# Local head attention on one core: the last block's odd score tiles masked on TensorE and gathered by a maximum

## The chip, the cores and the metric

One core of one Trainium2 chip runs the whole program in one launch. The metric is the device time in microseconds (us). The engines are named as the profile names them: PE (TensorE; PEld is its weight load), DVE (VectorE), ACT (ScalarE), POOL (GpSimd) and SP (SyncE, which here only issues DMAs).

## The reference, cut to what matters

The program computes two transformer layers: attention against a context, a mixture of experts, a second attention and a feed-forward. Only the second attention matters here. It does not attend over the sequence: for each of 2048 tokens, each of 16 heads (32 wide) attends to the 16 heads of the same token.

```python
B, S, D, H = (4, 1024, 512, 16)
HD = D // H
bs, sl, nf = q.shape
Q = (q @ Wq.T + bq).reshape(bs, sl, H, HD)
K = (k @ Wk.T + bk).reshape(bs, sl, H, HD)
V = (v @ Wv.T + bv).reshape(bs, sl, H, HD)
score = jnp.einsum('bshd,bsgd->bshg', Q, K)
weight = jax.nn.softmax(score, axis=-1)
attn = jnp.einsum('bshg,bsgd->bshd', weight, V).reshape(bs, sl, nf)
return attn @ Wo.T + bo
```

## The kernel before, in words

Four stages follow each other: `l0_attention`, `l0_experts`, `l1_attention` and `l1_output_ffn`, each a block of five instruction streams that ends with all engines joined. The change lies in `l1_attention`, the merged stage: it projects K, V and Q and does the attention in the same loop.

The tokens are cut into NBLK = 4 blocks of 512. A block has NP = 8 pairs of units, so there are 32 pairs, p = 0 to 31. A unit is one quarter of the block (a quadrant of 32 partitions, which holds the 32 features of a head) and UN = 4 groups of TOK = 8 tokens. For one group, a matmul over 32 rows multiplies 8 tokens x 16 heads of queries by 8 tokens x 16 heads of keys: a 128 x 128 tile, of which only the entries with the same token are wanted, one in eight. The two units of a pair lie in two neighbouring quadrants and write two PSUM banks, `sc_ps[:, 0]` and `sc_ps[:, 1]`, the even and the odd tile, each 128 x 512.

The stream of each engine is written out by hand. For pair p:

- PE, `scores(p)` (L2140): eight matmuls of 32 rows, even and odd in turn. They wait for the masking of both tiles of pair p-1, since there is one pair of banks. Then come half of a projection, `turn` (L2149, eight transposes of the probabilities of pair p-2), the other half of a projection, and `weigh` (L2162, pair p-3).
- DVE, `own_scores(2p)`: multiply the even tile by the 0/1 mask (L2248), then sum over the 8 tokens (L2254), which leaves 16 scores per row. Then `normalise(p-1)` (L2266 sum, L2268 reciprocal, L2270 scaling), then `own_scores(2p+1)` for the odd tile, then `subtract_max(p)` (L2259, L2261).
- ACT: the exponentials (L2024) and the copies of the turned probabilities and of the outputs out of PSUM.
- POOL, `expand(2p-2)` and `expand(2p-1)` (L1931): spread the normalised weights back to a 128 x 512 tile.

Beside blocks 0 to 2, that is beside pairs 0 to 23, PE also does the projections of the next block; some of these items need DVE too (`h_low_part`, L2223, and `take_v`, L2230). Beside the last block's pairs, 24 to 31, there are none. Pair 24 waits for the last block's queries, which come back by DMA and are laid out by ACT (L2014).

In this kernel's profile the rows of `scores` show two records for each matmul: an fp32 product is issued as two, so eight matmuls are x16. A transpose is one record.

The wait that stands between DVE and PE, and the two instructions around it:

```python
if p:
    pe.wait_ge(s_masked, 2 * p)
...
dve.tensor_tensor(masked_sc[:], sc_ps[:, u % 2], mask..., ALU.mult).then_inc(s_masked, 1)
...
dve.tensor_reduce(own_sc[:, p % 3, u % 2], masked_sc..., AX.X, ALU.add).then_inc(s_gathered, 1)
```

Of the kernel before, what the change touches and what calls it, by code (L numbers as in the profile page):

```python
# [14 lines left out]
P = 128  # L15
F32 = mybir.dt.float32
F32R = mybir.dt.float32r
I32 = mybir.dt.int32
ALU = mybir.AluOpType
ACT = mybir.ActivationFunctionType  # L20
AX = mybir.AxisListType
# [1529 lines left out]
def l1_attention(nc, new_sem, x_shared, expert_out, place, weight, carry, ctxT, W, w_ffn, woT, x2, qT, kT, vT, aT, sums):  # L1551
    T, D = x2.shape
    KC = D // P
    NBLK = T // BLK
    HD = 32
# [9 lines left out]
    RING = 6  # L1565
    TURN_LAG, LAG = 2, 3
# [20 lines left out]
    WHICH = {"k": 0, "v": 1, "q": 2}  # L1587

# [8 lines left out]
    with ExitStack() as c:  # L1597
        def sb(name, shape, dt=F32):
            return c.enter_context(nc.sbuf_tensor("p_" + name, shape, dt))

        def sem(name):
            return new_sem("p_" + name)
# [28 lines left out]
        ones = sb("ones", [P, P])  # L1631
        mhalf = sb("mhalf", [P, 1])
# [3 lines left out]
        masked_sc = sb("masked_sc", [P, UN, P])  # L1636
        own_sc = sb("own_sc", [P, 3, 2, UN, H])
# [42 lines left out]
        s_masked = sem("s_masked")  # L1680
        s_gathered = sem("s_gathered")
# [218 lines left out]
        def _(pool):  # L1900
# [40 lines left out]
            for n in range(TPB):  # L1941
                gather(n)
            for n in range(TPB):
                w_low("q", n)
                power(n)
# [136 lines left out]
        def _(pe):  # L2082
# [46 lines left out]
            def scores(p):  # L2129
                b, w = p // NP, p % NP  # L2130
                if w == 0:
                    pe.wait_ge(k_in[b % 2], IN_QK * (b // 2 + 1))
                    pe.wait_ge(q_moved, b + 1)
                if p:
                    pe.wait_ge(s_masked, 2 * p)
                for y in range(UN):
                    for u in (2 * w, 2 * w + 1):
                        rows = slice(u % NQ * HD, (u % NQ + 1) * HD)
                        n = u // NQ * UN + y
                        mm = pe.matmul(sc_ps[:, u % 2, y, :], q_laid[rows, b % 2, n],  # L2140
                                       k_sb[rows, b % 2, :, n * TOK:(n + 1) * TOK], start=True, stop=True)
                mm.then_inc(s_ready, 1)
# [39 lines left out]
        def _(dve):  # L2182
# [59 lines left out]
            def own_scores(u):  # L2242

                p = u // 2
                dve.wait_ge(s_ready, p + 1)
                if u:
                    dve.wait_ge(s_gathered, u)
# [5 lines left out]
                dve.wait_ge(s_masked, u + 1)  # L2253
# [10 lines left out]
            def normalise(p):  # L2264
# [6 lines left out]
                                  ALU.mult).then_inc(e_done, 1)  # L2271

# [39 lines left out]
            for p in range(NP * NBLK):  # L2312
# [13 lines left out]
                item_part(2 * p + 1)  # L2326
                for m in pieces_beside(p, "dve"):
                    sum_piece(m)
# [513 lines left out]
```

## Time and profile before

| | us |
|---|---|
| median of 3 runs | 2047.57 (2047.14 to 2050.84) |
| the profiled execution's own time | 2048.61 |
| its span, first to last instruction | 2046.8 |
| PE busy | 1918.5 (94% of the span) |
| DVE busy | 987.4 (48%) |
| last block's pairs, first score to end of the stage's PE work | 1678.6 to 1723.6 |

Busy shares are averages over four stages with different limits. The stretch that the change touches is about 45 us of 2047, so it is read by itself: which engine waits for which in it.

### The profile page before, as it was taken

Reading aid. Unit: us, or ns where it says so; the run is one execution under the profiler, and the core shown is the slowest. Engines: PE = TensorE matmul, PEld = TensorE weight load, DVE = VectorE, ACT = ScalarE, POOL = GpSimd, SP = SyncE. Lnnn points to the kernel's source line nnn. Section 1 sums busy time; section 2 is a strip of 40 time slices with the busy share of each in tenths; the row PEclk is TensorE's granted clock in tenths of the full one; section 3 lists DMA queues with packets and bytes.
Section 4 is the critical chain, followed back from the end, with each engine's and each line's share of the span. In section 5 each row is a group of like instructions: output and inputs, shape, how many; then the busy total and the mean of one; then the engine's idle time right before and its main releaser. Section 6 shows DMA issues by size and latency. Waiting matters only on the chain. (4 is left out here: it accounts for less than half of the span.)

```text
span 2046.8 us, 29418 instructions
## 1 busy us (share of the span) xinstructions
PE 1918.5 (94%) x10300; PEld 1608.7 (79%) x10300; DVE 987.4 (48%) x1657; ACT 752.6 (37%) x1144; POOL 1114.2 (54%) x996
## 2 busy tenths in 40 slices
PE   6999999999999999979999799998989896899998
PEld 5889888988898888857777699997767774678886
DVE  2447444745465545653332133334778866782111
ACT  3336333633345332622121222212445544343433
POOL 6775688648855876444117845640544424843333
PEclk9999999999999999979999899999989998999999
DMA  4231332223222323334126655532888655430000
GB/s 150 103 113 53 114 107 99 73 78 131 101 81 84 124 103 103 125 118 161 49 101 230 219 167 173 148 105 79 243 250 220 189 143 163 141 114 31 20 20 20
DMA packets 172235, 248.10 MB, mean 121 GB/s; under 512 B 44944, under 2 KB 69520, under 8 KB 172112
## 3 DMA queue, kind: packets, MB, share of 16 engines
q1 hardware_dynamic: 157024, 202.09, 31.1%
q0 software_dynamic: 9472, 34.09, 5.1%
q10 hardware_dynamic: 5616, 10.23, 1.3%
q8 instruction: 85, 1.39, 0.3%
q14 instruction: 38, 0.31, 0.1%
HBM read 179.77 MB, written 66.58 MB: 120 GB/s over the span
## 5 line engine op out<-in xcount | busy, mean ns | idle before, releaser
L257 POOL TENSOR_TENSOR a_w_hl<-a_w_raw,a_w_hl 128x512 fp32r<-128x512 f32 x236 | 312.7, 1357 | 142.9 <-ACT a_w_hl L330 142.7
L455 PE MATMUL a_proj<-a_c_hl,a_w_hl 128*128 128x512 f32 x768 | 179.8, 394 | 21.8 <-DVE a_w_hl L576 19.9
L455 PEld LDWEIGHTS a_proj<-a_c_hl,a_w_hl 128*128 128x128 f32 x768 | 144.4, 189 | 53.4 <-issue 21.5
L455 PE MATMUL a_proj<-a_w_hl,a_c_hl 128*128 128x512 f32 x768 | 181.2, 392 | 0.0
L529 PE MATMUL a_proj<-a_w_hl,a_a_hl 128*128 128x512 f32 x768 | 178.5, 391 | 0.0
L455 PE MATMUL a_proj<-a_a_hl,a_w_hl 128*128 128x512 f32 x768 | 176.4, 390 | 0.0
L330 ACT ACTIVATE a_w_hl<-a_w_raw 128x2048 fp32r<-128x2048 f32 x60 | 114.8, 1914 | 152.0 <-PE a_proj L455 106.7
L356 ACT ACTIVATE a_sq<-a_proj,a_vecs 128x512 f32<-128x512 f32 x128 | 88.2, 691 | 218.6 <-PE a_proj L455 136.6
L455 PEld LDWEIGHTS a_proj<-a_a_hl,a_w_hl 128*128 128x128 f32 x768 | 143.6, 188 | 29.7
L2530 POOL TENSOR_TENSOR f_a_hl<-f_act_sb,f_a_hl 128x512 fp32r<-128x512 f32 x64 | 86.0, 1344 | 148.6 <-ACT f_a_hl L2578 148.5
L529 PEld LDWEIGHTS a_proj<-a_w_hl,a_a_hl 128*128 128x128 f32 x768 | 143.0, 188 | 29.0
L455 PEld LDWEIGHTS a_proj<-a_w_hl,a_c_hl 128*128 128x128 f32 x768 | 142.4, 188 | 28.6
L1316 PE MATMUL b_gate_up<-b_wts,b_xt_hl 128*128 x936 | 160.0, 327 | 4.2 <-DVE b_xt_hl L1525 4.2
L1316 PEld LDWEIGHTS b_gate_up<-b_wts,b_xt_hl 128*128 128x128 f32 x936 | 155.2, 191 | 8.2 <-issue 5.0
L288 POOL TENSOR_TENSOR a_ssum<-a_ssum,a_sq 128x512 f32<-128x512 f32 x112 | 145.5, 1299 | 28.4 <-ACT a_sq L356 21.3
L1222 PE MATMUL b_gate_up<-b_wts 128*128 128x512 f32 (+1 forms) x576 | 136.0, 394 | 0.0
L1931 POOL TENSOR_TENSOR p_probs<-p_own_sc,p_mask 128x512 f32<-128x512 f32 x64 | 67.8, 1081 | 108.9 <-DVE p_own_sc L2270 107.7
L1222 PEld LDWEIGHTS b_gate_up<-b_wts 128*128 128x128 f32 (+1 forms) x576 | 102.9, 179 | 29.4
L2638 PE MATMUL f_totals<-f_ternary,f_a_hl 128*128 128x512 f32 x512 | 122.5, 396 | 0.0
L2624 PE MATMUL f_hidden<-f_h_hl,f_ternary 128*128 x512 | 120.4, 393 | 0.0
L2638 PEld LDWEIGHTS f_totals<-f_ternary,f_a_hl 128*128 128x128 f32 x512 | 96.4, 188 | 23.3
L632 DVE SCALAR_TENSOR_TENSOR a_a_hl<-a_qT,a_vecs,a_a_hl 128x512 fp32r<-128x512 f32 x64 | 67.4, 1068 | 96.3 <-ACT a_a_hl L370 96.3
(258 smaller groups left out, 3523.8 us busy)
## 6 DMA issues: line engine op xcount, KB each, us to landing
a_w_raw<-in_a_ki_w SPq DMA_DIRECT2D x16, 1024.0 KB, 5.6
a_w_raw<-in_a_vi_w SPq DMA_DIRECT2D x16, 1024.0 KB, 4.9
a_w_raw<-in_a_q_w SPq DMA_DIRECT2D x16, 1024.0 KB, 4.9
a_w_raw<-in_a_o_w SPq DMA_DIRECT2D x16, 1024.0 KB, 5.3
spare<-in_b_gate_up POOLq DMA_DIRECT2D x32, 352.0 KB, 4.1
l_sorted_rows<-b_zeros SPq DMA_DIRECT2D x39, 256.0 KB, 3.2
spare<-l_sorted_rows SPq DMA_DIRECT2D x39, 256.0 KB, 3.2
l_expert_out<-spare ACTq DMA_DIRECT2D x39, 256.0 KB, 3.5
```

Of the source, the lines that this page charges most:

```text
L257: ins = pool.tensor_tensor(w_hl[:, s, 1, k], w_raw[:, s, k], f32(w_hl[:, s, 0, k]), ALU.subtract)
L288: pool.tensor_tensor(ssum[:], first, sq[:, n % 2, :], ALU.add).then_inc(sq_added, 1)
L330: act.activation(w_hl[:, i % 2, 0], w_raw[:, i % 2], ACT.Copy).then_inc(w_high, 1)
L356: act.activation(sq[:, n % 2, :], proj[:, j, :], ACT.Square, bias=bias)\
L455: mm = pe.matmul(proj[:, j, :], left, right, start=(k == 0 and n == 0), stop=(k == KC - 1 and n == 2))
L529: mm = pe.matmul(proj[:, j, :], a_hl[:, ap, k, j * P:(j + 1) * P], w_hl[:, i % 2, wp, k], start=(n == 0 and m == 0), stop=(n == 4 * G - 1 ...
L1222: mm = pe.matmul(gu_ps[0:w, n, part, :], gu_hl[:, s, wp, k, cols], h_hl[:, hslot, ap, k, :], start=(k == 0 and m == 0), stop=(k == KC - 1 ...
L1316: mm = pe.matmul(gu_ps[:, i % 2, half, 0:F], x_part(i, xp)[:, own], part(r, P, at, F), start=(k == 0 and xp == 0 and start == HI), stop=(k ...
L1931: pool.tensor_tensor(probs[:, u % RING].rearrange("p y (g t) -> p y g t", t=TOK), own_sc[:, p % 3, u % 2].unsqueeze(3).to_broadcast([P, UN ...
L2530: pool.tensor_tensor(a_hl[:, 1, m % FC, :], act_sb[:, m % 2, :], f32(a_hl[:, 0, m % FC, :]), ALU.subtract).then_inc(g_split, 1)
L2624: mm = pe.matmul(h_ps[:, m % 2, :], w_t[:, 2 * g, k, f * P:(f + 1) * P], h_hl[:, ap, k, bass.ds(BLK * t, BLK)], start=(k == 0 and ap == 0) ...
L2638: mm = pe.matmul(y_ps[:, j, :], a_hl[:, ap, f, j * P:(j + 1) * P], w_t[:, 2 * g + 1, f, :], start=(m == 0 and ap == 0), stop=(m == NG * FC ...
```

## The change

From pair 24 on (`LEAN = NP * (NBLK - 1)`), the pairs that have no projections beside them, the odd tile is masked by PE. After the two score matmuls of a group, a third one adds `same_tok` x `not_tok` to the odd tile: over the 32 rows of that quadrant it adds 0 where the tokens agree and -1e30 where they do not (only 8 of the 32 rows of `same_tok` are not zero). DVE then needs no multiplication for the odd tile: one maximum over the 8 tokens, read straight from PSUM, gives the 16 scores. PE's next scores wait for that maximum (`s_gathered`) in place of the multiplication (`s_masked`). The even tile is treated as before. The two constant tiles are made in unused room: POOL writes row numbers early in the stage, and DVE makes the rest in four instructions behind pair 16.

```diff
+    LEAN = NP * (NBLK - 1)
...
+        low_row, low_flag = ones[:, 0:1].bitcast(I32), ones[:, 1:2]
...
+        same_tok, not_tok = (routed[:, 0, r, 0:P] for r in range(2))
...
+            pool.wait_ge(const_made, 4)
+            pool.iota(low_row, pattern=[[0, 1]], base=0, channel_multiplier=1).then_inc(off_tok, 1)
...
-                if p:
+                if p > LEAN:
+                    pe.wait_ge(s_gathered, 2 * p)
+                elif p:
                     pe.wait_ge(s_masked, 2 * p)
+                if p == LEAN:
+                    pe.wait_ge(off_tok, 5)
...
-                                       k_sb[rows, b % 2, :, n * TOK:(n + 1) * TOK], start=True, stop=True)
+                                       k_sb[rows, b % 2, :, n * TOK:(n + 1) * TOK], start=True,
+                                       stop=p < LEAN or u % 2 == 0)
+                    if p >= LEAN:
+                        mm = pe.matmul(sc_ps[:, 1, y, :], same_tok[rows], not_tok[rows], start=False, stop=True)
...
+                if p >= LEAN and u % 2:
+                    dve.wait_ge(p_ready, 2 * (p - 3) + 2)
+                    dve.tensor_reduce(own_sc[:, p % 3, 1], sc_ps[:, 1].rearrange("p y (g t) -> p y g t", t=TOK),
+                                      AX.X, ALU.max).then_inc(s_gathered, 1)
+                    return
...
-                dve.wait_ge(s_masked, u + 1)
+                dve.wait_ge(s_masked, u + 1 if p < LEAN else LEAN + p + 1)
...
+            def make_off_tok():
+                dve.wait_ge(off_tok, 1)
+                dve.tensor_scalar(low_row, low_row, HD - TOK, None, ALU.bitwise_and).then_inc(off_tok, 1)
+                dve.wait_ge(off_tok, 2)
+                dve.tensor_scalar(low_flag, low_row, 0.0, None, ALU.is_equal).then_inc(off_tok, 1)
+                dve.wait_ge(off_tok, 3)
+                as_rows = mask[:].rearrange("p h t -> p (h t)")
+                dve.tensor_scalar(same_tok, as_rows, low_flag, None, ALU.mult).then_inc(off_tok, 1)
+                dve.tensor_scalar(not_tok, as_rows, 1.0, BIG, ALU.subtract, ALU.mult).then_inc(off_tok, 1)
...
+                if p == LEAN - NP:
+                    make_off_tok()
```

DVE's order in the last block, before: two tiles with the same two instructions each, `normalise` between them.

```order
L2248 TENSOR_TENSOR p_masked_sc<-p_scores,p_mask 128x512
L2254 TENSOR_REDUCE p_own_sc<-p_masked_sc 128x64
L2266 TENSOR_REDUCE p_den<-p_own_sc 128x8
L2268 RECIPROCAL p_rden<-p_den 128x8
L2270 TENSOR_TENSOR p_own_sc<-p_own_sc,p_rden 128x128
L2248 TENSOR_TENSOR p_masked_sc<-p_scores,p_mask 128x512
L2254 TENSOR_REDUCE p_own_sc<-p_masked_sc 128x64
L2259 TENSOR_REDUCE p_mx<-p_own_sc 128x8
L2261 TENSOR_TENSOR p_own_sc<-p_own_sc,p_mx 128x128
```

The same place after the change (the numbers are lines of the changed file).

```order
L2267 TENSOR_TENSOR p_masked_sc<-p_scores,p_mask 128x512
L2273 TENSOR_REDUCE p_own_sc<-p_masked_sc 128x64
L2285 TENSOR_REDUCE p_den<-p_own_sc 128x8
L2287 RECIPROCAL p_rden<-p_den 128x8
L2289 TENSOR_TENSOR p_own_sc<-p_own_sc,p_rden 128x128
L2262 TENSOR_REDUCE p_own_sc<-p_scores 128x64
L2278 TENSOR_REDUCE p_mx<-p_own_sc 128x8
L2280 TENSOR_TENSOR p_own_sc<-p_own_sc,p_mx 128x128
```

One of nine instructions is gone; the one that frees the odd bank, L2262, stands where the multiplication stood. DVE's order behind pair 16, after the change:

```order
L2237 TENSOR_TENSOR p_a_hl<-p_proj,p_a_hl 128x4x128 x2
L2294 TENSOR_SCALAR p_ones<-p_ones 128x1
L2296 TENSOR_SCALAR p_ones<-p_ones 128x1
L2299 TENSOR_SCALAR p_routed<-p_mask,p_ones 128x128
L2300 TENSOR_SCALAR p_routed<-p_mask 128x128
L2267 TENSOR_TENSOR p_masked_sc<-p_scores,p_mask 128x512
```

The four middle instructions are new; before, pair 17's mask (the last row) came right behind `h_low_part` (the first row). PE's order in one pair of the last block, after the change; before, there was one row `p_scores<-p_k,carry` with x8, and nothing with `p_routed`.

```order
L2151 MATMUL p_scores<-p_k,carry 128x128 x2
L2155 MATMUL p_scores<-p_routed 128x128
L2151 MATMUL p_scores<-p_k,carry 128x128 x2
L2155 MATMUL p_scores<-p_routed 128x128
L2151 MATMUL p_scores<-p_k,carry 128x128 x2
L2155 MATMUL p_scores<-p_routed 128x128
L2151 MATMUL p_scores<-p_k,carry 128x128 x2
L2155 MATMUL p_scores<-p_routed 128x128
```

Four matmuls of 32 rows are added to each of eight pairs, in the odd tile's quadrant, between the even and odd ones of the next group.

## Rows read from the trace of the kernel before

**Rows 1.** Windows: length, busy of PE, PEld, DVE, ACT, POOL (count); granted clock; DMA.

```profile
1679.00:1689.00 10.00, 10.00 (x72) 8.21 (x72) 6.76 (x15) 4.67 (x13) 2.50 (x3) 0.50 0.63 175
1690.80:1713.20 22.40, 16.50 (x205) 13.34 (x204) 20.67 (x47) 10.32 (x26) 10.54 (x10) 1.00 0.56 163
```

**Rows 2.** Timeline, DVE, pair 28: start us, us, what, [idle before].

```profile
1699.75 0.68 DVE L2248 TENSOR_TENSOR p_masked_sc<-p_scores,p_mask 128x512 f32<-128x512 f32 x1
1700.53 0.69 DVE L2254 TENSOR_REDUCE p_own_sc<-p_masked_sc 128x64 f32<-128x512 f32 x1
...
1701.90 0.68 DVE L2248 TENSOR_TENSOR p_masked_sc<-p_scores,p_mask 128x512 f32<-128x512 f32 x1
1702.68 0.69 DVE L2254 TENSOR_REDUCE p_own_sc<-p_masked_sc 128x64 f32<-128x512 f32 x1
...
1704.23 0.68 DVE L2248 TENSOR_TENSOR p_masked_sc<-p_scores,p_mask 128x512 f32<-128x512 f32 x1
```

**Rows 3.** Timeline, PE, pairs 29 and 30.

```profile
1702.63 1.16 PE L2140 MATMUL p_scores<-p_k,carry 32*128 32x128 f32 x16 [1.25 <-DVE p_masked_sc L2248]
1703.73 1.15 PE L2149 MATMUL p_turned<-p_ident,p_probs 128*128 128x128 f32 x8
1704.81 1.07 PE L2162 MATMUL p_out<-p_probs,p_v 128*32 128x128 f32 x16
1707.11 1.16 PE L2140 MATMUL p_scores<-p_k,carry 32*128 32x128 f32 x16 [1.24 <-DVE p_masked_sc L2248]
```

**Rows 4.** Timeline, DVE and PE, pair 21: scores and the mask behind them.

```profile
1659.45 0.69 DVE L2248 TENSOR_TENSOR p_masked_sc<-p_scores,p_mask 128x512 f32<-128x512 f32 x1 [0.77 <-PE p_scores L2140]
...
1658.24 1.16 PE L2140 MATMUL p_scores<-p_k,carry 32*128 32x128 f32 x16
```

**Rows 5.** Timeline, PE, `l0_attention`: fp32 matmuls of all 128 rows, one after another.

```profile
838.40 1.06 PE L516 MATMUL a_proj<-a_probs,carry 128*128 128x128 f32 x8
839.30 1.06 PE L495 MATMUL a_scores<-spare,a_qT 128*128 128x128 f32 x8
```

**Rows 6.** Timeline, PE, pairs 24 to 26, the start of the last block.

```profile
1678.61 1.87 PE L2140 MATMUL p_scores<-p_k,carry 32*128 32x128 f32 x16 [2.53 <-issue]
...
1684.16 2.08 PE L2140 MATMUL p_scores<-p_k,carry 32*128 32x128 f32 x16
1686.17 1.97 PE L2149 MATMUL p_turned<-p_ident,p_probs 128*128 128x128 f32 x8
```

**Rows 7.** Timeline, DVE, even masks of pairs 24, 25 and 26.

```profile
1680.52 0.69 DVE L2248 TENSOR_TENSOR p_masked_sc<-p_scores,p_mask 128x512 f32<-128x512 f32 x1 [4.03 <-PE p_scores L2140]
...
1686.29 0.69 DVE L2248 TENSOR_TENSOR p_masked_sc<-p_scores,p_mask 128x512 f32<-128x512 f32 x1 [1.20 <-PE p_scores L2140]
...
1690.79 0.68 DVE L2248 TENSOR_TENSOR p_masked_sc<-p_scores,p_mask 128x512 f32<-128x512 f32 x1
```

**Rows 8.** Groups, DVE, whole span: busy us, mean ns, idle before.

```profile
L642 DVE TENSOR_REDUCE a_mx<-a_scores 128x4 f32<-128x512 f32 x64 | 43.9, 686 | 5.7 <-PE a_scores L495 5.7
L2254 DVE TENSOR_REDUCE p_own_sc<-p_masked_sc 128x64 f32<-128x512 f32 x64 | 43.9, 686 | 6.2
```

**Rows 9.** Groups as in 8: small operations like the four new ones.

```profile
L2209 DVE TENSOR_SCALAR p_rstd<-p_mv 128x1 f32<-128x1 f32 x16 | 2.5, 154 | 0.6
L2283 DVE TENSOR_SCALAR p_mask<-p_flag 128x128 f32<-128x128 f32 x1 | 0.2, 228 | 0.0
```

**Rows 10.** Timeline, PE and DVE, pairs 17 and 18.

```profile
1636.06 2.99 PE L2125 MATMUL p_proj<-p_a_hl,p_w_hl 128*128 128x512 f32 x12 [2.70 <-DVE p_a_hl L2223]
...
1628.54 0.69 DVE L2223 TENSOR_TENSOR p_a_hl<-p_proj,p_a_hl 128x512 fp32r<-128x512 f32 x1 [0.26 <-ACT p_a_hl L1997]
1629.31 0.69 DVE L2248 TENSOR_TENSOR p_masked_sc<-p_scores,p_mask 128x512 f32<-128x512 f32 x1
```

**Rows 11.** Timeline, the tail: pair 31's even mask and its spreading.

```profile
1713.19 0.68 DVE L2248 TENSOR_TENSOR p_masked_sc<-p_scores,p_mask 128x512 f32<-128x512 f32 x1
...
1719.06 2.11 POOL L1931 TENSOR_TENSOR p_probs<-p_own_sc,p_mask 128x512 f32<-128x512 f32 x2 [1.46 <-DVE p_own_sc L2270]
```

More of the change, by code:

```diff
@@ L1565, in l1_attention @@
     RING = 6
+    BIG = 1e30
     TURN_LAG, LAG = 2, 3
@@ L1680, in l1_attention @@
         s_masked = sem("s_masked")
+        off_tok = sem("off_tok")
         s_gathered = sem("s_gathered")
```

## The prediction

> **What bounds the kernel now.** The program ends on TensorE's work in its last stage, so a delay or a saving in the merged stage moves the whole time only if it moves that stage's end. It does: the next stage starts when all engines have joined, and nothing of it overlaps. So I read the last block's pairs, 24 to 31, alone. First the windows: from 1690.80 to 1713.20, five periods of a pair, DVE is busy 20.67 of 22.40 us and PE 16.50, at a granted clock of 1.00 (2.4 GHz) [rows 1]. Then the timeline of one pair: on DVE the even mask starts at 1699.75, the odd at 1701.90, the next pair's even mask at 1704.23, so a pair takes 4.48 us, with no idle time in brackets [rows 2]. On PE the scores wait 1.25 and 1.24 us for DVE [rows 3]. DVE sets the pace, and PE's wait costs nothing, because the scores of the next pair (start 1702.63) are done before DVE is back at 1704.23. That overlap is what the reader should keep in view: PE starts 0.73 us after the odd mask starts, and DVE then still has the sum, the maximum and the subtraction to do, 1.55 us from 1702.68 to 1704.23.
>
> The block begins otherwise. From 1679 to 1689 the granted clock was 0.50 (1.2 GHz) with PE busy all 10.00 us [rows 1]; pair 24's scores start at 1678.61, pair 25's at 1684.16 [rows 6], and DVE waits for PE, 4.03 and 1.20 us. There PE is the bound. Even masks start at 1680.52, 1686.29 and 1690.79 [rows 7].
>
> **The change, part by part.**
>
> *The multiplication of the odd tile goes.* DVE's own work per pair falls by the step from the odd mask to the sum, 1701.90 to 1702.68, or 0.78 us [rows 2], to 3.70. If DVE stayed the bound that would be a gain of 8 x 0.78 = 6.2 us.
>
> *The maximum from PSUM.* No row of this stage reads PSUM with a reduction, but the first attention does: 686 ns, the same as the sum from SBUF [rows 8]. I take 0.69. The Trainium skill, VectorE: DVE Perf Modes, section on the TRN2 errata, gives a PSUM source 62 cycles more than an SBUF source; worked out at its 0.96 GHz that would be an estimate of 0.06 us more per pair, 0.5 us in eight. The rows show no difference, so I leave it out.
>
> *The wait moves.* The odd bank was free when the mask ended; now it is free when the maximum ends. The maximum stands where the mask stood, 2.15 us behind the even mask, and has the same length, so PE's scores start at the same place, 2.15 + 0.74 = 2.89 us behind the even mask. But what DVE has left to do after that has shrunk by the 0.78, to about 0.8 us, and PE now needs longer. The scores are no longer hidden, and the two engines take turns: a loop of DVE (2.89), then PE, then DVE.
>
> *PE's part.* From the start of the scores to the even mask behind them, where DVE was waiting, it is 1659.45 - 1658.24 = 1.21 us [rows 4]. The four added matmuls are two records each. What a record costs in one row group is seen in the first attention: eight records, 838.40 to 839.30, so 0.112 us each [rows 5]. Sixteen records of scores take 1.10 us to the next operation [rows 3], which is possible only if the two quadrants run side by side, two records at a time. The added records all fall to the odd quadrant, behind the two they add to. In program order the even quadrant can fill only one of their places, as it filled one of the odd scores' before. So eight more places, 8 x 0.112 = 0.90 us per pair. At the lower clock twice that, 1.79: sixteen score records there take 2.01 us to the next operation, against 1.10 [rows 6, 3].
>
> *The steady loop:* 2.89 + 1.21 + 0.90 = 5.00 us against 4.48, so 0.52 more for each of the five steps from pair 26 to 31: +2.6 us. PE's own work is 1.10 + 1.08 + 1.07 [rows 3] + 0.90 = 4.15 us, so it does not bind by itself.
>
> *The four DVE instructions behind pair 16.* 0.154 twice and 0.228 twice [rows 9] with some 0.03 us for each wait: 0.9 us. Pair 17's mask follows `h_low_part` at 1629.31 with no idle time before it, and PE then waits 2.70 us for DVE's `h_low_part` at 1636.06 [rows 10]. Behind that PE is the bound up to the queries of block 3, on which pair 24 waits. So I count the whole 0.9 as a shift of pair 24, to 1679.51. Low bound 0, if something else comes last there. The row numbers on POOL are one instruction of 128x1 ahead of work that waits for DVE; I count nothing, at most 0.2.
>
> *The start of the block.* Pair 24: mask at 1679.51 + 1.91 + 1.79 = 1683.21. PE, busy without a gap, starts pair 25 after 5.55 + 1.79 us, at 1686.85. If the clock comes back at about 1689.1 as before, 2.3 of the 3.92 us (2.13 + 1.79) are at the low clock and the rest costs half: mask 25 at 1690.0. Then the loop: scores 26 at 1692.9, mask 26 at 1695.0. Before it was 1690.79, so +4.2 us, with the 0.9 in it.
>
> *The end.* Pair 31's even mask comes at 1713.19 + 4.2 + 2.6 = 1720.0. From there to the spreading on POOL it was 5.87 us [rows 11]; the missing multiplication makes it 0.78 shorter. What follows is as before.
>
> **Sum:** +4.2 + 2.6 - 0.8 = +6.0 us. Against the profiled execution's own 2048.61 us that is 2054.6; the median of the runs lies 1.04 lower, so 2053.6 us, slower by 0.29%. A measurement of this kernel can tell about 0.2%, 4.1 us, from no change.
>
> **Bounds of PE's part.** It is the one large unknown. Lower: an added matmul costs half, 0.45 us per pair; then the loop is 4.55 (+0.3 in all), mask 26 comes at 1693.5 (+2.7), and the end is +2.2, or 2049.8. Upper: the two quadrants stop overlapping, 24 records of 0.112 in place of eight places, +1.8 us per pair; loop 5.9, and the end is some +13, or 2061. I take 0.90, which is counted from the nearest rows on both sides.
>
> **The rivals.**
>
> - *PE hides the mask (not slower).* At the place where DVE waits for `s_ready`, all hangs on how much longer the scores take. If they grow by less than 0.38 us per pair, the loop (4.10 + that) is shorter than 4.48. At nothing added, mask 26 comes +0.5, five steps give -1.9, the end -0.8: -2.2 us, 2045.4. For it: the rows show two quadrants side by side, and the even one stands idle while the odd is masked. Against it: the added work is all in one quadrant, whose sixteen records need 16 x 0.112 = 1.79 us whatever the other does. Even DVE as the sole bound (3.70) gives only about -4 us, since the block's start is PE's.
> - *The clock comes back earlier.* In the low stretch PE was already busy 10.00 of 10.00 us, so more matmuls cannot fill a gap; but they put other work in it. If pair 25's scores run at the full clock, mask 25 comes 1.0 us earlier: +5.0, or 2052.6. It is in my range. The Trainium skill, TensorE: Matmul & The Clock Gate, Part 1, says that the throttled state is the default and that activity releases it; by that rule a denser stage leans this way, never to a gain against before.
> - *Overlap lost (slower by far).* 2061, as above. Nothing in the rows speaks for it except that three matmuls in a row now change quadrant unevenly.
> - *The masking does not happen in time.* Pair 24 waits for the constants, but the order has them behind pair 16, some 50 us earlier; no cost.
>
> **How the numbers follow.** My forecast, DVE and PE in turns at about 5.0 us a pair, 0.62; an earlier clock 0.12; a cheaper mask between 0 and the lower bound 0.16, of which the greater part ends within 0.2%; overlap lost 0.06; other effects of either sign, the next stage's clock among them, 0.04. Range: 2049.5 to 2058. Its low end takes in the lower bound; its high end is 4.4 us above the sum, which is a third of the way to the lost overlap, 0.6 us more per pair. Outside are most of the lost overlap and the fully hidden mask. Slower by over 0.2% (above 2051.7) 0.76, within 0.2% 0.20, faster 0.04.
>
> **What the profile after would show.** Right: in the last block L2262 takes 0.69 us; PE's scores are x24, 2.0 us at the full clock, and start with DVE as their releaser; DVE has a new idle time of about 1.3 us per pair before the even mask, ended by PE scores; the masks are 5.0 us apart. Wrong: masks 4.5 us or less apart, or no idle time of DVE there, would say that the added matmuls ran beside the others. Pair 24 starting at the old place, measured from pair 16, would say that the four instructions were hidden.

## The result, and the profile after

| | before | after |
|---|---|---|
| median, us | 2047.93 (2047.14 to 2050.84, 6 runs) | 2057.59 (2055.31 to 2063.09, 6 runs) |
| ratio, 95% interval | | 1.0044 [1.0034, 1.0054] |
| profiled execution, its time | 2048.61 | 2055.76 |
| its span | 2046.8 | 2054.0 |
| PE busy | 1918.5 | 1928.0 |
| DVE busy | 987.4 | 979.4 |

The change made the kernel slower: 9.7 us between the medians, 9.0 us by the ratio with an interval of about 7 to 11 us, and 7.15 us between the two profiled executions. The ratios, here and below, are worked out over the fast executions alone, without the few slow ones (up to 7242 us), and are not the quotients of the medians. DVE works 8 us less and the program takes longer. The median came out 4 us above the predicted 2053.6 and inside the range, close to its high end.

First the windows of the kernel after: from pair 26's even mask to pair 31's, then the low stretch at the block's start, then a short stretch inside the block (columns as in [rows 1]).

```profile
1695.40:1720.91 25.51, 21.86 (x241) 18.74 (x242) 16.48 (x40) 9.87 (x23) 10.78 (x10) 0.93 0.61 186
1681.10:1688.00 6.90, 6.85 (x44) 6.18 (x46) 2.82 (x7) 2.38 (x6) 0.71 (x1) 0.51 0.51 116
1705.00:1708.40 3.40, 3.40 (x21) 2.71 (x22) 2.67 (x6) 1.56 (x4) 0.53 (x1) 0.50 0.66 159
```

Against [rows 1], DVE fell from 20.67 of 22.40 us to 16.48 of 25.51, PE rose from 16.50 to 21.86, and neither is busy all the time. That is how two engines look when they wait for each other in turn. The clock shows 0.93 where before it was 1.00; the last row is the reason, and it returns below.

DVE's timeline of the kernel after, the pairs that answer to [rows 2]:

```profile
1695.40 0.69 DVE L2267 TENSOR_TENSOR p_masked_sc<-p_scores,p_mask 128x512 f32<-128x512 f32 x1 [1.45 <-PE p_scores L2155]
...
1700.38 0.69 DVE L2267 TENSOR_TENSOR p_masked_sc<-p_scores,p_mask 128x512 f32<-128x512 f32 x1 [1.45 <-PE p_scores L2155]
...
1702.54 0.69 DVE L2262 TENSOR_REDUCE p_own_sc<-p_scores 128x64 f32<-128x512 f32 x1
1703.26 0.29 DVE L2278 TENSOR_REDUCE p_mx<-p_own_sc 128x8 f32<-128x128 f32 x1
...
1705.55 0.69 DVE L2267 TENSOR_TENSOR p_masked_sc<-p_scores,p_mask 128x512 f32<-128x512 f32 x1 [1.63 <-PE p_scores L2155]
```

Even masks are 4.98 us apart (1695.40 to 1700.38) where they were 4.48. The odd maximum L2262 starts 2.16 us behind the even mask and takes 0.69 us, as the odd mask did. Before, none of the masks in [rows 2] had a bracket; now each even mask has one that ends with PE's scores, 1.45 us where the clock is full.

PE's timeline beside it, which answers to [rows 3]; a record x5 is scores, the next line is the mask matmul behind them:

```profile
1698.29 0.59 PE L2151 MATMUL p_scores<-p_k,carry 32*128 32x128 f32 x5 [0.91 <-DVE p_own_sc L2262]
...
1699.96 0.38 PE L2155 MATMUL p_scores<-p_routed 32*128 32x128 f32 x2
1700.28 1.09 PE L2163 MATMUL p_turned<-p_ident,p_probs 128*128 128x128 f32 x8
1701.30 1.07 PE L2176 MATMUL p_out<-p_probs,p_v 128*32 128x128 f32 x16
...
1703.28 0.59 PE L2151 MATMUL p_scores<-p_k,carry 32*128 32x128 f32 x5 [0.92 <-DVE p_own_sc L2262]
```

From the first score to the turning behind it, 1698.29 to 1700.28, is 1.99 us, against 1.10 in [rows 3]: 0.89 us more. And PE, which is now the later one, itself waits 0.91 us for DVE's odd maximum. From the even mask to PE's scores it is 2.89 us, and from those to the next even mask 2.09, together 4.98: a pair is one lap of a chain that goes once through each engine.

Where the four constants are made, DVE (answers to [rows 10]):

```profile
1629.20 0.69 DVE L2237 TENSOR_TENSOR p_a_hl<-p_proj,p_a_hl 128x512 fp32r<-128x512 f32 x1 [0.26 <-ACT p_a_hl L2004]
1629.81 0.14 DVE L2294 TENSOR_SCALAR p_ones<-p_ones 128x1 int32<-128x1 int32 x1
1629.98 0.15 DVE L2296 TENSOR_SCALAR p_ones<-p_ones 128x1 f32<-128x1 int32 x1
1630.17 0.29 DVE L2299 TENSOR_SCALAR p_routed<-p_mask,p_ones 128x128 f32<-128x128 f32 x1
1630.37 0.22 DVE L2300 TENSOR_SCALAR p_routed<-p_mask 128x128 f32<-128x128 f32 x1
1630.51 0.68 DVE L2267 TENSOR_TENSOR p_masked_sc<-p_scores,p_mask 128x512 f32<-128x512 f32 x1
```

The mask starts 1.31 us behind `h_low_part` instead of 0.77 [rows 10]: the four instructions delay it by 0.54 us, not by 0.9, because their ends overlap. Last, PE and DVE of the kernel after from pair 18 to the start of the block (answers to [rows 10, 6, 7]):

```profile
1637.26 4.35 PE L2132 MATMUL p_proj<-p_a_hl,p_w_hl 128*128 128x512 f32 x12 [2.70 <-DVE p_a_hl L2237]
...
1681.15 0.98 PE L2151 MATMUL p_scores<-p_k,carry 32*128 32x128 f32 x5 [2.52 <-issue]
...
1684.97 0.69 DVE L2267 TENSOR_TENSOR p_masked_sc<-p_scores,p_mask 128x512 f32<-128x512 f32 x1 [5.94 <-PE p_scores L2155]
...
1690.41 0.69 DVE L2267 TENSOR_TENSOR p_masked_sc<-p_scores,p_mask 128x512 f32<-128x512 f32 x1 [1.89 <-PE p_scores L2155]
```

Pair 24's scores start 2.54 us later than before (1678.61 [rows 6]), and only 0.54 of that belongs to the four instructions. `h_low_part` ahead of them already starts 0.66 us late (1629.20 against 1628.54), and pair 18's projection took 4.35 us in place of 2.99, since a stretch of low clock fell on it: 1.36 us. So differences between two single profiles carry an error of a microsecond or more. At pair 26's even mask the delay is 4.61 us (1695.40 against 1690.79), at pair 31's 7.72 (1720.91 against 1713.19 [rows 11]), and the program's end is 7.2 us later.

### The profile page after: what moved, and what is told of

Read it like the earlier page. It is cut to its first block and busy times, and to the rows that moved or that the text cites. A ratio compares the mean times of both kernels' runs of the same rounds, so it can differ in the third digit from the quotient of the medians.

```text
span 2054.0 us, 29535 instructions
## 1 busy us (share of the span) xinstructions
PE 1928.0 (94%) x10364; PEld 1618.9 (79%) x10364; DVE 979.4 (48%) x1653; ACT 752.8 (37%) x1144; POOL 1120.0 (55%) x997
```

## The experiments

Each ran beside the kernel before on the same chip; the ratios are against those runs. The medians of before were 2047.93 beside the change; 2048.07 beside constants alone, matmuls only, no matmuls and constants late; 2047.30 beside matmuls twice and the three bf16 kernels; 2048.65 beside the other four. **Lap** is the distance between even masks (or even maxima) at the full clock. **Five steps** runs from the maximum over the heads (`p_mx`) of pair 26 to that of pair 31, and **low** is how much of it was at the granted clock 0.50. Kernels that make the constants "late" make them behind pair 23 in place of pair 16.

| kernel | lap | five steps | low | median, us | ratio, 95% interval |
|---|---|---|---|---|---|
| before | 4.48 | 22.41 | 0 | 2047.93 | |
| constants alone | 4.48 | 22.41 | 0 | 2047.99 | 1.0003 [0.9993, 1.0013] |
| the change | 4.98 | 25.52 | 3.4 | 2057.59 | 1.0044 [1.0034, 1.0054] |
| the change again | 4.98 | 26.13 | 6.8 | 2056.05 | 1.0040 [1.0026, 1.0054] |
| matmuls only | 4.98 | 26.14 | 6.8 | 2056.69 | 1.0044 [1.0031, 1.0057] |
| constants late | 4.98 | 25.96 | 3.5 | 2053.15 | 1.0036 [1.0022, 1.0051] |
| same quadrant, other bank, late | 4.98 | 25.51 | 3.4 | 2052.80 | 1.0019 [1.0005, 1.0032] |
| matmuls twice | 5.87 | 35.01 | 20.5 | 2066.82 | 1.0093 [1.0068, 1.0118] |
| no matmuls | 4.10 | 20.50 | 0 | 2046.22 | 0.9989 [0.9980, 0.9998] |
| other quadrant, other bank, late | 4.12 | 22.42 | 3.4 | 2045.43 | 0.9982 [0.9969, 0.9994] |
| odd tile in bf16, late | 4.48 | 22.36 | 0 | 2048.74 | 1.0008 [0.9993, 1.0023] |
| both tiles in fp32, late | 4.20 | 21.02 | 0 | 2045.94 | 0.9987 [0.9977, 0.9998] |
| both tiles in bf16, late | 3.68 | 24.54 | 10.2 | 2043.83 | 0.9980 [0.9968, 0.9991] |
| both tiles in bf16, wide, late | 3.52 | 17.58 | 0 | 2041.90 | 0.9970 [0.9956, 0.9983] |

### The parts alone: constants, matmuls, moved wait

The constants alone, on top of the kernel before:

```diff
-    LEAN = NP * (NBLK - 1)
+    LEAN = NP * NBLK
...
-                if p == LEAN - NP:
+                if p == LEAN - 2 * NP:
```

> The kernel before with the constant tiles alone: POOL's row numbers and DVE's four instructions behind pair 16, no added matmul, no maximum, no moved wait. My theory: DVE's 0.8 to 0.9 us go onto the path of pair 17 and 18, PE's wait for DVE before the projection stays 2.7 us and comes 0.9 us later, and pair 24 starts 0.9 us later; the loop of the last block stays 4.48 us; in all +0.9 us, some 2048.8. Rival, the four instructions are hidden: pair 24 at the old distance from pair 16 and no change. Rival, the clock: the shift puts other work in a stretch at the lower clock, and pair 24 comes 2 us or more later in some execution though the instructions take 0.9.

Measured: no difference that can be told from zero, 1.0003 [0.9993, 1.0013]. The timeline has the same 0.5 us of delay for pair 17, and here too pair 18's projection took 4.37 us at the low clock, with the block unchanged. The 0.5 us, and the expected 0.9, lie inside that interval (-1.4 to +2.7 us), so they are neither shown nor excluded in the total. The constants' place is not what made the change lose 9 us.

The mask matmuls alone, from pair 24 (`MASKED`) on, with DVE doing all its old work (the multiplication then acts on an already masked tile):

```diff
-                                       stop=p < LEAN or u % 2 == 0)
-                    if p >= LEAN:
+                                       stop=p < MASKED or u % 2 == 0)
+                    if p >= MASKED:
```

> The changed kernel with DVE's old work: the mask matmuls are added to the odd tile, but DVE multiplies it by the mask and sums as before, and PE waits for the multiplication (the output is the same, since -1e30 is multiplied by 0). My theory (DVE and PE in turns): PE starts 2.88 us behind the even mask and needs 2.11, so the masks are 4.99 us apart, as in the changed kernel, DVE idles some 0.5 us per pair in place of 1.45, and only the end is later, by 0.78 us: some 0.8 us above the changed kernel, 2058.4. Rival, DVE's saved instruction is worth its length in every pair: 8 x 0.78 = 6.2 us above the changed kernel, 2063.8, masks 5.8 us apart.

DVE's timeline of this kernel:

```profile
1694.36 0.69 DVE L2268 TENSOR_TENSOR p_masked_sc<-p_scores,p_mask 128x512 f32<-128x512 f32 x1 [1.58 <-PE p_scores L2156]
...
1696.51 0.68 DVE L2268 TENSOR_TENSOR p_masked_sc<-p_scores,p_mask 128x512 f32<-128x512 f32 x1
...
1699.34 0.69 DVE L2268 TENSOR_TENSOR p_masked_sc<-p_scores,p_mask 128x512 f32<-128x512 f32 x1 [0.41 <-PE p_scores L2156]
```

The lap is 4.98 us, the same as in the full change, and the ratio is the same 1.0044. DVE has 0.78 us more to do per pair and still waits, 0.41 us. Taking that instruction away turned work into idle time and saved nothing per pair: it stands behind the release of PE and beside PE's scores. The 0.8 us at the end that were expected on top of the change are less than these runs can tell (median 2056.69 against 2057.59 and 2056.05).

The other half alone, the odd maximum and the moved wait without the matmuls:

```diff
-                    if p >= LEAN:
-                        mm = pe.matmul(sc_ps[:, 1, y, :], same_tok[rows], not_tok[rows], start=False, stop=True)
```

> The changed kernel without the mask matmuls: the odd tile's maximum is taken over unmasked scores, so the masking of the odd tile is left out. The wait stands where the change put it. My theory: the masks are 2.89 + 1.21 = 4.10 us apart, DVE idles some 0.4 us per pair, and the end is 2 us before the kernel before: 2045.7. Rival, the moved wait costs by itself: masks 4.5 us apart or more, 2048 or above. Rival, the low clock and not the matmuls makes the loss: still above 2050.

```profile
1692.22 0.69 DVE L2265 TENSOR_TENSOR p_masked_sc<-p_scores,p_mask 128x512 f32<-128x512 f32 x1 [0.56 <-PE p_scores L2151]
...
1696.32 0.69 DVE L2265 TENSOR_TENSOR p_masked_sc<-p_scores,p_mask 128x512 f32<-128x512 f32 x1 [0.56 <-PE p_scores L2151]
```

This kernel leaves the odd tile unmasked; only its time counts. DVE's timeline shows a lap of 4.10 us, which is 2.89 + 1.21, and even here DVE waits 0.56 us. So the wait for the maximum costs nothing, and the largest gain that this rearrangement could have had at no price for PE is 0.38 us a pair. The matmuls are the loss, 0.88 us a pair.

### The constants late

```diff
-                if p == LEAN - NP:
+                if p == LEAN - 1:
```

> The changed kernel with DVE's four constant instructions behind pair 23, where DVE idles 4 us or more before pair 24. My theory: pair 24's scores start at the old 1678.6 (from the same start of the stage), and the whole is 0.9 us shorter than the changed kernel in its mechanism, some 2056.7; the loop stays 4.98. Rival, the four instructions were hidden where they stood: no difference. Rival, the clock: since the changed kernel's profile has 1.36 us lost to a low clock in a projection of pair 18, removing the shift could give back 2.3 us, 2055.3.

Measured: 1.0036 [1.0022, 1.0051], lap 4.98. The interval overlaps those of the change, so what the constants' place is worth stays below what these runs can tell.

### What an added matmul costs: doubled, moved, narrowed

Each mask matmul issued twice:

```diff
-                        mm = pe.matmul(sc_ps[:, 1, y, :], same_tok[rows], not_tok[rows], start=False, stop=True)
+                        for last in (False, True):
+                            mm = pe.matmul(sc_ps[:, 1, y, :], same_tok[rows], not_tok[rows], start=False, stop=last)
```

> The changed kernel with every mask matmul issued twice (the mask becomes -2e30; the output is the same). My theory: eight more places of 0.112 us in the odd quadrant, so the masks are 4.98 + 0.90 = 5.88 us apart at the full clock; DVE idles 2.35 us per pair; in all some 8 us above the changed kernel (five loops of 0.9, the rest at the block's start at the lower clock), near 2066. Rival, only the first mask matmul's latency counts, or the second runs beside the even quadrant: less than 0.5 us more per pair, under 2062.

```profile
1690.19 0.69 DVE L2268 TENSOR_TENSOR p_masked_sc<-p_scores,p_mask 128x512 f32<-128x512 f32 x1 [3.26 <-PE p_scores L2156]
...
1696.06 0.69 DVE L2268 TENSOR_TENSOR p_masked_sc<-p_scores,p_mask 128x512 f32<-128x512 f32 x1 [2.34 <-PE p_scores L2156]
```

DVE's timeline: 5.87 us, again 0.89 more, and DVE's wait grew by the same 0.89, from 1.45 to 2.34. Over none, four and eight added matmuls (laps 4.10, 4.98, 5.87) the price is linear in their number. The median of 2066.82 us is the expected 2066, but this profile also has 20.5 us of low clock in its five steps.

Is it a price of the quadrant, of the PSUM bank, or of a matmul as such? Two kernels write the same product into a bank that the last block does not use, so both leave the odd tile unmasked. One takes the rows of a quadrant without scores, as in this cut; the other keeps the odd tile's quadrant:

```diff
-                        mm = pe.matmul(sc_ps[:, 1, y, :], same_tok[rows], not_tok[rows], start=False, stop=True)
+                        off = slice((u + 2) % NQ * HD, ((u + 2) % NQ + 1) * HD)
+                        mm = pe.matmul(proj[:, 0, y * P:(y + 1) * P], same_tok[off], not_tok[off], start=True, stop=True)
```

> The four mask matmuls of a pair are issued as in the change, but on the rows of a quadrant that holds no scores of this pair, and they write a PSUM bank that the last block does not use (the projections'), so their product reaches nothing: the odd tile's maximum is unmasked. The constants are made behind pair 23. My theory is that the 0.90 us is the queue in one quadrant, not a cost of the matmuls as such: eight records in a third quadrant then run beside the other sixteen, PE's part falls back to about 1.21 us, and the loop is 2.89 + 1.21 = 4.10 us, as without the mask matmuls, at most 0.2 more; total near 2046. Rival: a matmul costs its place wherever it stands (only two run side by side, or the issue is the limit), so the loop stays 4.98 us and the total near 2053 to 2056.

> As the kernel with the other quadrant, but on the odd tile's own quadrant, still into the unused PSUM bank; the odd tile's maximum is unmasked and the constants are made behind pair 23. It differs from the change only in the bank that the mask matmuls write and in that they add to nothing. My theory, a queue in one quadrant: loop 4.98 us, total near 2053. Rival, the cost is that of adding to a bank that was just written: a different bank then takes it away, and the loop is near 4.10 us.

PE's timeline with the other quadrant:

```profile
1708.08 0.38 PE L2151 MATMUL p_scores<-p_k,carry 32*128 32x128 f32 x2 [0.83 <-DVE p_own_sc L2263]
1708.10 0.37 PE L2156 MATMUL p_proj<-p_routed 32*128 32x128 f32 x1
1708.30 0.28 PE L2151 MATMUL p_scores<-p_k,carry 32*128 32x128 f32 x2
...
1709.18 1.09 PE L2164 MATMUL p_turned<-p_ident,p_probs 128*128 128x128 f32 x7
```

And with the odd tile's own quadrant, also on PE:

```profile
1695.74 0.59 PE L2151 MATMUL p_scores<-p_k,carry 32*128 32x128 f32 x5 [0.91 <-DVE p_own_sc L2263]
...
1697.42 0.38 PE L2156 MATMUL p_proj<-p_routed 32*128 32x128 f32 x2
1697.73 1.09 PE L2164 MATMUL p_turned<-p_ident,p_probs 128*128 128x128 f32 x8
```

In the other quadrant, 24 records take 1.10 us from the first score to the turning, exactly what 16 took before [rows 3]: three run at a time, the mask record starting 0.02 us behind the scores'. The lap is 4.12 us and the kernel is faster than before. In the same quadrant, with the bank changed, the scores take 1.99 us to the turning and the lap stays at 4.98 us. So the 0.89 us is the queue in one quadrant. It is neither a price of adding to a bank nor one of issuing a matmul. The Trainium skill, TensorE: Matmul & The Clock Gate, Part 3 (The mechanism), has matmuls on distinct row groups run concurrently and end in program order. The trace agrees with the first half, by the 24 records in 1.10 us; it can't show the second, since the ends of matmuls in these profiles are modelled. The third quadrant may not be able to serve the change itself, which has to add to the odd tile's own bank. The Trainium skill, TensorEngine Tiling (Array Packing), Gotcha 1, says that different row tiles cannot access the same PSUM bank at once; no run here tried that.

The constants as bf16 make a mask matmul one record in place of two (late, odd tile alone):

```diff
-        same_tok, not_tok = (routed[:, 0, r, 0:P] for r in range(2))
+        same_tok, not_tok = (routed[:, 0, r, 0:P // 2].bitcast(BF16) for r in range(2))
```

> The changed kernel with the two constant tiles in bf16 (0, 1 and -1e30 lose nothing that matters), and made behind pair 23. The mask matmul is then one record of half the length. My theory, places filled strictly in program order: a mask matmul still waits for the odd scores and holds back the next even ones, so it takes one place of 0.112 in place of two: 0.45 us per pair, masks 4.54 us apart, the whole about 1.5 us above the kernel before, 2049.6. Rival, only its own length counts (0.056 each): 4.32 us apart, and under the kernel before by 0.5 us. Rival, the number of matmuls counts and not their length: 4.98.

```profile
1696.33 0.59 PE L2152 MATMUL p_scores<-p_k,carry 32*128 32x128 f32 x5 [0.91 <-DVE p_own_sc L2263]
...
1697.66 0.21 PE L2156 MATMUL p_scores<-p_routed 32*128 32x128 bf16 x1
1697.81 1.09 PE L2164 MATMUL p_turned<-p_ident,p_probs 128*128 128x128 f32 x8
```

PE's scores take 1.48 us to the turning: four bf16 matmuls cost 0.38 us, or 0.095 each, where the fp32 ones cost 0.22 each. That is neither the one place of 0.112 that was expected nor the rival's 0.056, but nearer to the place. The lap is 2.89 + 1.59 = 4.48, equal to the kernel before by coincidence, and so is the time: 1.0008 [0.9993, 1.0023]. This is the break-even of the idea for one tile, and it lies where the prediction's rival had put it, 0.38 us a pair.

### Both tiles masked on PE

If the price is places in one quadrant, the even tile's mask matmuls should be free beside the odd ones, and DVE would lose both multiplications:

```diff
-                    if p >= LEAN:
-                        mm = pe.matmul(sc_ps[:, 1, y, :], same_tok[rows], not_tok[rows], start=False, stop=True)
+                    if p >= LEAN:
+                        for u in (2 * w, 2 * w + 1):
+                            rows = slice(u % NQ * HD, (u % NQ + 1) * HD)
+                            mm = pe.matmul(sc_ps[:, u % 2, y, :], same_tok[rows], not_tok[rows], start=False, stop=True)
```

> Both tiles are masked by fp32 matmuls of 32 rows and gathered by a maximum, constants made behind pair 23. DVE loses both multiplications (its own work 2.92 us a pair); the even tile's mask matmuls fall into places that stand open in the change beside the odd ones, so PE's part stays 1.21 + 0.90 = 2.11 us. The odd maximum starts 0.69 + 0.68 = about 1.37 us behind the even one and ends 0.69 later, so the loop is about 2.10 + 2.11 = 4.2 us against 4.98 in the change and 4.48 before: total near 2047 to 2050, since the block's start is PE's. Rival: the even mask matmuls cost places of their own, 0.90 more, so the loop is 5.1 us and the total 2054 or more.

DVE's timeline, two even maxima:

```profile
1699.86 0.69 DVE L2264 TENSOR_REDUCE p_own_sc<-p_scores 128x64 f32<-128x512 f32 x1 [1.46 <-PE p_scores L2157]
...
1704.06 0.69 DVE L2264 TENSOR_REDUCE p_own_sc<-p_scores 128x64 f32<-128x512 f32 x1 [1.46 <-PE p_scores L2157]
```

4.20 us, as expected, and 0.9987 [0.9977, 0.9998]. The median of 2045.94 us lies a microsecond under the 2047 to 2050 that were expected. There are four more fp32 matmuls a pair than in the change and no more time on PE: 1.98 us from the first score (1697.76) to the turning (1699.74). The same with bf16 constants:

> Both tiles masked on PE with bf16 constants (made behind pair 23), a mask matmul per tile and group; DVE takes two maxima from PSUM and multiplies nothing. My theory: the even mask fills places that stand open, so PE's part grows by 0.45 us as in the kernel with the odd tile alone, while the wait for the second maximum comes 0.78 us earlier: DVE 2.10 + PE 1.66 = 3.76 us per pair against 4.48 before; the end 1.6 us shorter; the block's start up to 2 us later; in all 3 us before the kernel before, 2045. Rival, PE's own work becomes the bound (3.25 + 0.45 = 3.70): about the same. Rival, two more matmuls per group cost as much as one more each: loop 4.2 and no gain.

Measured 0.9980 [0.9968, 0.9991], with a lap of 3.68 us (even maxima at 1712.78 and 1716.46). PE's scores start 3.68 us apart (1711.20 and 1714.88) with no bracket, so PE's own work sets the pace, as the rival had it, and not the turns of 3.76 us. Its five steps are long in the table since this profile has 10.2 us of low clock in them.

Last, one 512-column matmul per tile in place of four. Only the first group of a tile starts its bank afresh; the others and the mask add to it:

```diff
-                                       k_sb[rows, b % 2, :, n * TOK:(n + 1) * TOK], start=True,
+                                       k_sb[rows, b % 2, :, n * TOK:(n + 1) * TOK], start=p < LEAN or y == 0,
...
+                        mm = pe.matmul(sc_ps[:, u % 2], same_tok[rows],
+                                       not_tok[rows].unsqueeze(1).to_broadcast([HD, UN, P]), start=False, stop=True)
```

> Both tiles masked on PE by one bf16 matmul each that covers the four groups (512 columns, -1e30 pattern repeated by a zero step), behind the eight score matmuls; only the first group's score matmul starts a new accumulation of the bank. My theory: the two wide matmuls run side by side, 0.22 us per pair; loop 2.10 + 1.43 = 3.53 us, with PE's own work at 3.47 just under it; in all 5 to 6 us before the kernel before, 2042.5. Rival, they run one after the other: 0.44, loop 3.75, 2045.

PE's timeline of this kernel:

```profile
1697.17 1.16 PE L2152 MATMUL p_scores<-p_k,carry 32*128 32x128 f32 x16
1698.17 0.38 PE L2158 MATMUL p_scores<-p_routed 32*128 32x512 bf16 x2
1698.48 1.09 PE L2167 MATMUL p_turned<-p_ident,p_probs 128*128 128x128 f32 x8
1699.50 1.07 PE L2180 MATMUL p_out<-p_probs,p_v 128*32 128x128 f32 x16
1700.69 0.49 PE L2152 MATMUL p_scores<-p_k,carry 32*128 32x128 f32 x4
```

And DVE's:

```profile
1698.59 0.69 DVE L2266 TENSOR_REDUCE p_own_sc<-p_scores 128x64 f32<-128x512 f32 x1 [0.77 <-PE p_scores L2158]
...
1702.11 0.69 DVE L2266 TENSOR_REDUCE p_own_sc<-p_scores 128x64 f32<-128x512 f32 x1 [0.77 <-PE p_scores L2158]
```

From the first score to the turning it is 1.31 us (1697.17 to 1698.48) where the scores alone took 1.10: the two wide mask matmuls run side by side and add 0.21. The lap is 3.52 us and PE has no bracket left: the chain of turns is gone and PE's own work sets the pace. Median 2041.90, ratio 0.9970 [0.9956, 0.9983]: faster than both kernels.

### The change once more

> The change once more, unaltered, beside the others of this call: its times and granted clocks settle how much of the 9.6 us between the medians belongs to the chip's clock on the day. My steps give +6.0; the two profiled executions lie 7.2 apart. Expected 2054 to 2058, loop 4.98 us where the clock is full. If the low-clock stretch inside the last block (1705 in the first profile) is chance, it is not there again at the same place; if it follows from the denser block, one lies between pairs 26 and 31 again.

Windows of three stretches of low clock, one at the block's start and two inside it:

```profile
1683.10:1696.80 13.70, 13.70 (x91) 11.48 (x90) 6.60 (x16) 4.88 (x13) 4.31 (x4) 0.50 0.62 174
1703.60:1707.00 3.40, 3.40 (x26) 2.49 (x26) 3.10 (x8) 1.21 (x3) 1.27 (x2) 0.50 0.02 5
1713.90:1717.30 3.40, 3.40 (x25) 2.83 (x24) 3.08 (x8) 1.19 (x2) 1.01 (x1) 0.50 0.87 233
```

Measured: 1.0040 [1.0026, 1.0054]. Two low stretches lie between pairs 26 and 31, and the one at the block's start is twice as long as in the first profile. The block's length from pair 24's `p_mx` to pair 31's is 39.72 us here, 35.94 in the first profile, 32.67 in the kernel before. The lap is the same in both profiles of the change; the clock makes the 3.8 us between them.

Every execution has its mean granted clock on record, over the whole program, and that reaches further than single profiles:

| kernel | executions | mean granted clock |
|---|---|---|
| before, beside two sets of the kernels below | 57 | 0.9743 |
| the change, both measurements | 17 | 0.9718 |
| matmuls only | 6 | 0.9712 |
| constants late | 7 | 0.9729 |
| same quadrant, other bank, late | 9 | 0.9743 |
| both tiles in fp32, late | 12 | 0.9760 |

The change ran at a lower clock, by 0.0025, against a standard error of 0.0006. Each microsecond at 0.50 takes half a microsecond off the mean, so as an estimate that is 10 us more at 0.50 in each execution (2 x 0.0025 x 2057). Its slow-clocked executions are also its long ones (2063.72 us at 0.968, 2055.31 at 0.975). A straight line through the 17 gives 1.1 us for each 0.001, and at the clock of before, 0.9743, some 2054.5 us: about 6.4 above the mean of before, 2048.15. This is a fit, not a run at that clock.

## Why the prediction was right, and where it was short

**The bound and the lap: right.** "The scores are no longer hidden, and the two engines take turns": 5.00 us was forecast, 4.98 measured, with the idle time on DVE (1.45 us, about 1.3 forecast) that the text named as the sign. The matmuls alone give the same lap, so it is shown that DVE's lost instruction is worth nothing there.

**PE's part: right in size and in reason.** Eight places of 0.112 us, 0.90; measured 0.89, doubled with twice the matmuls, gone in another quadrant, and unchanged with another bank. "The even quadrant can fill only one of their places" is what the kernel with both tiles in fp32 confirms from the other side: it fills them with the even masks at no cost (1.98 us to the turning, 1.99 in the change).

**The maximum from PSUM: right.** 683 to 685 ns in the eight of them, against 686 for the sum from SBUF [rows 8]. The Trainium skill, VectorE: DVE Perf Modes, in its section on the TRN2 errata, gives 62 cycles more for a PSUM source; they do not show here.

**The constants: overstated, and no loss that can be measured.** Forecast 0.9 us at pair 17; measured 0.54, and 1.0003 [0.9993, 1.0013] alone. The 2.54 us at pair 24 in the profile of after misleads: 0.66 was there ahead of the four instructions, and 1.36 is the low clock on pair 18's projection. The kernel with the constants alone had the same low stretch there (4.37 us) without losing time in the end, and the kernel with the constants late had it too (4.58 us) without the instructions, so they do not bring it.

**The sum: 6.0 us, too small.** By their ratios the two measurements of the change give 9.0 us (7.0 to 11.1) and 8.2 (5.3 to 11.1); the first excludes 6.0, the second does not. Against the profile of before, step by step:

| step | forecast | first profile | second profile |
|---|---|---|---|
| even mask of pair 26 | +4.2 | +4.61 | +7.63 |
| even masks 26 to 31 | +2.6 | +3.11 | +3.72 |
| even mask 31 to the last spreading on POOL | -0.8 | -1.02 | -1.02 |
| even mask 31 to the end of the last `p_out` | -0.8 | +0.14 | -1.01 |

The step that fell short is the clock. The prediction took one low stretch at the block's start that ends "at about 1689.1 as before", and the full clock from there on. In the profile of after the first stretch ended early, which helped, but another one came at 1705.0 in the middle of the block and made two laps 5.17 and 5.39 us long. In the second profile two came in the middle, and the one at the start was twice as long. The saving at the end came as forecast, and a little more; POOL's last spreading in the first profile of the change (answers to [rows 11]):

```profile
1720.91 0.69 DVE L2267 TENSOR_TENSOR p_masked_sc<-p_scores,p_mask 128x512 f32<-128x512 f32 x1 [1.45 <-PE p_scores L2155]
...
1725.76 2.11 POOL L1936 TENSOR_TENSOR p_probs<-p_own_sc,p_mask 128x512 f32<-128x512 f32 x2 [0.36 <-DVE p_own_sc L2289]
```

That is 4.85 us where it was 5.87 [rows 11]. In the first profile a third low stretch, from about 1725.5 to 1729, fell on the last matmuls and took the saving back. Together the stage ends 7.9 and 10.3 us later; the program ends 7.2 and 9.1 later, and the difference lies in the next stage. At the clock of before, the fit above leaves about 6.4 us, close to the 6.0 of the sum, and the kernel with the same lap whose clock was that of before (same quadrant, other bank, constants late) lost 3.9 us (1.0 to 6.6). So the missing 3 us are about the size of the clock's share; no run fixes the clock to show it.

**The range held partly by luck.** Its high end, 2058, was drawn for a dearer mask on PE, not for the clock, and the median of 2057.59 us lies just under it. It was also described wrongly: 4.4 us above the sum is 0.6 of the way to the 2061 of the lost overlap, not a third.

**The rival on the clock leaned the wrong way.** It had the denser PE bring the clock back sooner. In the rows and in the executions the added PE work came with more low clock, not less. The Trainium skill, TensorE: Matmul & The Clock Gate, Part 1, has activity release the throttled state; the 13.70 us at 0.50 with PE busy for all of them do not agree with a release that comes soon. Whether the added work causes the low clock stays open. For it: all five profiles with a lap of 4.98 us, and the one with 5.87, have low clock inside the five steps, the kernel before and the constants alone have none, and the mean clocks of the change and of the matmuls alone are lower. Against it: the kernel with both tiles in fp32 has PE busier still (20.37 us of 21.02), no low clock there and the highest mean clock; the wide bf16 one (17.01 of 17.58) has none either. The one with the other quadrant, with a lap of 4.12, has 3.4 us, and the narrow bf16 one, with 3.68, has 10.2. And the same quadrant with another bank does the same work on PE as the change at the mean clock of before, 0.9743.

**"PE hides the mask" was rightly rejected** for the change as it was written, and its threshold was right: the bf16 kernel sits on it. What it missed is that the even tile's mask matmuls run beside the odd one's, so that the even multiplication can go as well at no more time on PE (0.88 us a pair in fp32, 0.38 in bf16), and that one wide bf16 matmul a tile costs only 0.21.

## What to carry to other kernels

Before moving work from a busy engine to a less busy one, follow one lap of the chain between them and ask on which side of the hand-over each instruction stands. Here the instruction removed stood behind the hand-over, where it cost nothing, and the work added stood in front of the next one, where all of it counts. Count an added small matmul on TensorE by the row group it queues in: in these runs it was free beside a busy one and cost its full time in the same one. And do not trust a difference of a few microseconds between two single profiles: the mean clock of many executions showed here what two timelines could only suggest.

## What the runs showed that I had not expected

- In the first profile of the change the granted clock was 0.50 from 1705.00 to 1708.40, in the middle of a stretch where PE was busy 21.86 of 25.51 us; in the second it stayed at 0.50 for 13.70 us with PE busy all 13.70. Over executions, the clock of the change was lower too (0.9718 against 0.9743).
- Three fp32 matmuls of 32 rows in three quadrants take no longer than two (1.10 us for 24 records against 1.10 for 16).
- Small DVE instructions one behind the other cost less than the sum of their durations: four of 0.14, 0.15, 0.29 and 0.22 us delayed what follows by 0.54.
